# One-core attention block: where the rows of the stacked bf16 q and k are copied from, and where they lie

## The reference, cut to what matters

```python
x = L0_attn_x                                  # (4, 512, 256) f32
xn = _layernorm(x, axis=-1)
qkv = xn @ Wqkv.T + bqkv                       # 16 heads of 16
q, k, v = to_heads(...); q = _rope(q); k = _rope(k)
att = softmax(where(causal, q @ k.T / sqrt(16), -inf)) @ v
s = att @ Wo.T + bo
g = _silu(einsum('btd,rde->bte', xn, factors) / sqrt(8) + bias)
return x + s * g
```

## Time and profile before

| | |
|---|---|
| median of 3 runs | 281.85 us (279.93 to 281.97) |
| profiled execution, first to last instruction | 280.9 us |
| DMAs of 64 KB to stacks (L343) | 96, of which GpSimd issues 4 |
| DMAs of 128 KB within stacks (L380) | 48 |
| mean granted TensorE clock | 0.918 |

### The profile page before, as it was taken

One profiled execution on the slowest core, in us unless ns is written; L12 is line 12 of the kernel. 1 busy time (PEld: TensorE's weight loads), 2 busy tenths in 40 slices (PEclk: granted clock), 3 DMA queues, 4 the chain that ended last, 5 costly groups with the idle time before them and its releaser, 6 DMA issues.

```text
span 280.9 us, 4735 instructions
## 1 busy us (share of the span) xinstructions
PE 228.2 (81%) x1672; PEld 142.9 (51%) x1672; DVE 201.8 (72%) x623; ACT 139.3 (50%) x259; POOL 118.6 (42%) x85
## 2 busy tenths in 40 slices
PE   6480446878896999999599599997599989999992
PEld 2350333354463665556475375645467546675662
DVE  2879882988977699899657389899145898861125
ACT  1403240022493566598336345678025849748950
POOL 4065780643744413783070156575070890016000
PEclk9986586989999799999999869999599999999998
DMA  6970885830496780267598300067585000002002
GB/s 199 359 245 19 105 101 74 99 55 2 66 100 81 84 124 5 41 81 92 63 105 128 99 0 2 22 93 103 87 103 128 0 3 2 2 1 79 0 2 75
DMA packets 16407, 21.28 MB, mean 76 GB/s; under 512 B 2240, under 2 KB 14912, under 8 KB 15616
## 3 DMA queue, kind: packets, MB, share of 16 engines
q1 hardware_dynamic: 15936, 20.59, 43.6%
q0 software_dynamic: 192, 0.26, 0.7%
q10 hardware_dynamic: 256, 0.13, 0.3%
HBM read 6.16 MB, written 2.10 MB: 29 GB/s over the span
## 4 chain that ended last, share of the span: by engine, by line
PE 36%; DVE 20%; DMA 20%; SPq 13%; ACT 5%; issue 3%; ACTq 2%; DVEq 0%
DMA stack_k<-parts 9%; PE o_ps L416 8%; DVE ring_ps L687 8%; SPq L343 8%; DMA stack_k<-stack_k 7%; PE ring_ps L494 6%; PE ring_ps L470 5%; PE ring_ps L460 5%; SPq L380 4%; PE ring_ps L453 4%; ACT probs L786 3%; DMA xbuf<-x 2%; PE ring_ps L426 2%; PE ring_ps L504 2%; DVE rotated L667 2%
## 5 line engine op out<-in xcount | busy, mean ns | idle before, releaser
L687 DVE CUSTOM_DVE_ANT_0 ring_ps<-ring_ps,later_k 128x512 f32<-128x512 f32 (+3 forms) x224 | 107.1, 541 | 27.3 <-PE ring_ps L470 26.5
L786 ACT ACTIVATE probs<-ring_ps 128x512 f32<-128x512 f32 x160 | 85.6, 613 | 28.6 <-PE ring_ps L504 26.1
L470 PE MATMUL ring_ps<-stack_k,stack_q 96*128 96x512 bf16 (+3 forms) x256 | 64.3, 313 | 18.7 <-DMA stack_k<-stack_k 15.7
L494 PE MATMUL ring_ps<-stack_q,stack_k 98*128 98x512 bf16 (+3 forms) x256 | 60.7, 306 | 4.5 <-DVE rowmax L687 3.8
L470 PEld LDWEIGHTS ring_ps<-stack_k,stack_q 96*128 96x128 bf16 x256 | 22.9, 101 | 39.4 <-issue 22.9
L460 PE MATMUL ring_ps<-wvg_sb,xnT 128*128 128x512 f32 x96 | 32.4, 487 | 11.9 <-DVE wvg_sb L603 11.9
L504 PE MATMUL ring_ps<-ident_bf,later_k 128*128 128x256 bf16 (+1 forms) x160 | 40.8, 255 | 0.0
L416 PE MATMUL o_ps<-probs,vaug 128*17 128x256 f32 (+3 forms) x496 | 36.1, 430 | 0.5 <-ACT probs L786 0.4
L494 PEld LDWEIGHTS ring_ps<-stack_q,stack_k 98*128 98x128 bf16 x256 | 23.1, 99 | 18.3 <-DVE rowmax L687 8.6
L453 PE MATMUL ring_ps<-xnT,wqk_sb 128*128 128x512 f32 x96 | 27.8, 443 | 4.7 <-DVE xnT L612 4.7
L687 DVE DVE_READ_ACCUMULATOR2_ANT rowmax<- 128x1 f32 x224 | 31.3, 140 | 0.0
(11 more groups left out here) (84 smaller groups left out, 303.6 us busy)
## 6 DMA issues: line engine op xcount, KB each, us to landing
stack_q<-stack_q SPq DMA_DIRECT2D x24, 128.0 KB
stack_k<-stack_k SPq DMA_DIRECT2D x24, 128.0 KB
stack_q<-parts SPq DMA_DIRECT2D x46, 64.0 KB
stack_k<-parts SPq DMA_DIRECT2D x46, 64.0 KB
probs<-factors SPq DMA_DIRECT2D x2, 1024.0 KB, 9.7
out<-result SPq DMA_DIRECT2D x8, 256.0 KB, 3.4
xbuf<-x SPq DMA_DIRECT2D x3, 512.0 KB, 8.3
xbuf<-x SPq DMA_DIRECT2D x2, 256.0 KB, 2.9
```

The source lines that it names most:

```text
L470: mm = pe.matmul(ps[:, s * width:(s + 1) * width], qk[b % 2][0][0:DOT_ROWS, h, tile * P:(tile + 1) * P], qk[b % 2][1][0:DOT_ROWS, h, 0:width],
L494: pe.matmul(ps[:, col:col + T - j * P], qk[b % 2][1][0:ROWS, h, j * P:(j + 1) * P], qk[b % 2][0][0:ROWS, h, j * P:T], start=(n == 0), stop ...
L687: last = dve.tensor_tensor_reduce(scores, scores, later_k[:, T - width:], 1.0, LOWEST, ALU.add, ALU.max, rowmax[:, tile, h:h + 1])
L786: act.activation(probs[:, pair % PROB_SLOTS, i % EXP_CHUNKS, :], ps[:, :], ACT.Exp, scale=float(HD) ** -0.5).then_inc(taken[kind], 1)
```

## The change

All 12 blocks of 8 rows that a stack and unit have ("places", `PLACES = 12`) are copied from `parts`; nothing is copied from stack to stack. Where 8 rows of one place were adjacent, they are now four partitions apart: place 4g + r takes rows 32g + r, 32g + r + 4, ... 32g + r + 28. The order of the rows within the 96 changes alike for q and k, so the dot products are the same sums.

```diff
-STACK_DMAS = 2 * 5
+PLACES = len(Q_PARTS) * 2
+STACK_DMAS = 2 * PLACES
+def stack_rows(place):
+    first = 4 * HALF * (place // 4) + place % 4
+    return slice(first, first + 4 * (HALF - 1) + 1, 4)
...
-            row = STACKED_PARTS[n].index(part) * HD
-            if part < 2:
-                signal_of_place = s_placed[part]
-            else:
-                signal_of_place = s_stack[b % PARITIES][u] if (b, u) != (0, 0) else s_first_low
-            for half in range(2):
-                eng.dma_start(qk[b % PARITIES][n][row + half * HALF:row + (half + 1) * HALF,
-                                                  u * UH:(u + 1) * UH, :],
-                              parts[n * UR:(n + 1) * UR, u, part, half, :]
-                              ).then_inc(signal_of_place, 16)
+            placed = s_first_low if (b, u, part) == (0, 0, 2) else s_stack[b % PARITIES][u]
+            for product, held in enumerate(STACKED_PARTS[n]):
+                if held == part:
+                    for half in range(2):
+                        eng.dma_start(qk[b % PARITIES][n][stack_rows(2 * product + half), u * UH:(u + 1) * UH, :],
+                                      parts[n * UR:(n + 1) * UR, u, part, half, :]
+                                      ).then_inc(placed, 16)
...
-                    def repeat(n, part):
-                        sp.wait_ge(s_placed[part], 4 * 16 * (UNITS * b + i + 1))
-                        stack = qk[b % PARITIES][n][:, i * UH:(i + 1) * UH, :]
-                        first, *others = (g * HD for g, held in enumerate(STACKED_PARTS[n]) if held == part)
-                        for row in others:
-                            sp.dma_start(stack[row:row + HD], stack[first:first + HD]).then_inc(stacked, 16)
...
+                    for part in range(3):
+                        if (b, i, part) != (0, 0, 2):
+                            place(sp, b, i, 0, part)
+                            place(sp, b, i, 1, part)
```

More of the change, by code:

```diff
@@ L296, in block_kernel @@
         s_low = sem("low_ready")
-        s_placed = [sem("high_placed"), sem("middle_placed")]
         s_first_low = sem("first_low_placed")
@@ L371, in _ @@
                         sp.wait_ge(done_pe["scores"], count("scores", b - PARITIES, (i + 1) * UP * EXP_CHUNKS - 1))
-                    stacked = s_stack[b % PARITIES][i]
-                    def repeat(n, part):
-                        sp.wait_ge(s_placed[part], 4 * 16 * (UNITS * b + i + 1))
-                        stack = qk[b % PARITIES][n][:, i * UH:(i + 1) * UH, :]
-                        first, *others = (g * HD for g, held in enumerate(STACKED_PARTS[n]) if held == part)
-                        for row in others:
-                            sp.dma_start(stack[row:row + HD], stack[first:first + HD]).then_inc(stacked, 16)
[L382 to L392, removed]
+                    for part in range(3):
+                        if (b, i, part) != (0, 0, 2):
+                            place(sp, b, i, 0, part)
+                            place(sp, b, i, 1, part)
                 elif kind == "project_o":
```

## The result

The median is 263.84 us (four runs, 262.32 to 266.05), beside 280.89 us for the kernel before in the same session (278.00 to 281.97). The ratio is 0.9418, with a 95% interval of 0.9348 to 0.9488: 17.0 us faster. The forecast was 268.6 us. Ratios leave out a few disturbed executions, so they can differ by some thousandths from the quotient of two medians. The profiled execution has a span of 264.2 us and its own time is 266.05.

What follows compares the result with a forecast made beforehand. The prediction took slow filling of the stacks to bound the kernel, with PE waiting 15.7 us for them. A to E sum to 13.2 us: 280.9 to 267.7, plus 0.9 for the median, 268.6 us; range 262 to 279.

Steps and rivals of the forecast that it cites:

- The new copy: A 64 KB copy onto rows four apart: taken as 0.35 us, below SP's issue of 0.655 us; landing about 2.5 us.
- A: Unit (0, 0): stack complete at 40.3, 4.3 us earlier; worth 4.0 us, ends 2.7 and 4.3.
- B: Unit (1, 0): stack ready at 87.5, PE's whole gap of 2.26 closes; worth 2.2 us, ends 1.0 and 2.26.
- C: Unit (2, 0): PE's 3.20 us gap closes until VectorE is late next; worth 2.0 us, ends 1.2 and 3.2.
- D: Batch 3's x, issued after unit (2, 1)'s stacks, goes out 5.1 us earlier; worth 2.9 us, ends 1.5 and 3.07.
- worth nothing: Second units (u = 1): their stacks are ready earlier too, but no one waits for them; 0 us.
- E: Unit (3, 0): filling takes 17.6 us instead of 19.7; worth 2.1 us, ends 1.2 and 3.93, PE still waiting 1.8.
- The 0.9 us that tied the span to the median: Added to the 267.7 us forecast for the profiled execution to give the forecast median of 268.6 us.
- Rival 1: Every unit's copies stay as slow as a place, 0.9 us each: about 8.3 us slower, 290 us; chance 0.12.
- Rival 2: Gaps for stacks close but VectorE takes over; only A and E remain, 6.1 us: 275.7 us; chance 0.15.
- Rival 3: The change does nothing: a copy takes about 0.75 us or units keep their length; 281 to 282 us; chance 0.05.
- some 5 us: Sign expected in the new profile: batch 3's x goes out this long after unit (2, 1) could have ended.

Runs made afterwards that it cites:

- experiment 1: The changed kernel with each copy's 8 destination rows adjacent again, all copies still straight from `parts`: 300.13 us, ratio 1.0642.
- experiment 2: The kernel before with only the rows spread (a place's four apart, a product's two apart), stack-to-stack copies kept: 261.88 us, ratio 0.932.
- before, again: The kernel before, unchanged, run once more for a second profile: 284.03 us in one execution.
- 4, x early: The kernel before with only batch 3's x issued by GpSimd once the result is there, not by SP behind the stacks: 280.07 us, ratio 0.996.
- 6, second units: The change in the second units (u = 1) alone, first units filled as in the kernel before: 275.55 us, ratio 0.9803.
- 7, x held: The changed kernel with SP made to wait for the scores of unit (1, 1) before issuing batch 3's x: 264.22 us, ratio 0.9416.
- 5, first units: The change in the first units (u = 0) alone, second units filled as in the kernel before: 266.55 us, ratio 0.9496.
- after, again: The changed kernel, unchanged, run once more for a second profile: 265.12 us in one execution.
- experiment 8: The kernel of experiment 2 with VectorE's normalisation of batch 1 moved later, to after about 13 of unit (0, 0)'s 22 maxima: 259.37 us, ratio 0.9266.

## Why the prediction was right, and by how much it was off

**The mechanism held.** The step "what holds the repeats is where the bytes lie, not the number of engines" is what experiments 1 and 2 tell apart: the same DMAs with other destination rows give 300.1 or 263.8 us, and copies of copies with other rows give 280.9 or 261.9. For the repeats by themselves it is the 121 and 201 GB/s under experiment 2, with 16 outer rows in both.

The Trainium skill's SBUF — State Buffer (Door 1: The DMA port swizzle) gave an estimate of 1.2 us for eight adjacent rows and 0.3 for rows four apart; by the same rule rows two apart reach four ports, an estimate of 0.6 us. Measured are 0.83 to 0.98 us with adjacent rows, quicker than the page's estimate, and no more than SP's 0.655 at two and at four apart, where the copy itself is hidden; so the order is the page's, and the time of a spread copy was not measured. By the Trainium skill's DMA: Bandwidth & Descriptors (Why a DMA increments its semaphore by 16) a copy with eight outer rows uses eight engines and one with sixteen uses sixteen. That did not decide: the former now move 99 GB/s at a share of 0.35, the latter moved 121 at 1.11.

**The new copy.** "Any value below 0.655 us gives the same result" held: the issue is the pace. Landing was taken as 2.5 us and measured at 2.2 in steady state, 2.56 at the end of unit (0, 0). Unit (0, 0) was to be complete at 40.3 and is at 40.30; unit (3, 0) was to take 17.6 us and takes 17.8 (164.48 to 182.30).

**A and B.** Forecast 4.0 and 2.2, measured 4.97 and 2.64. The maxima of (0, 0) start 4.34 us earlier, the upper end of A. Another 0.8 us come from there to the first place of (1, 0), 24.37 us against 25.15. That is no more than executions of one kernel differ: the second profiles have 23.68 and 25.70, the longer one at a lower mean clock (0.74 against 0.78). In B the gap of 2.26 closed, and with it goes the stretch at the lower clock behind it, 91 to 95 us: PE's busy time there falls from 38.98 to 37.99 us.

**C and D, where a term was mis-sized:** 4.9 forecast, 7.83 measured. The working took D from PE's gap ("the gap of 3.07 is the limit: 2.9"), shortened C to 2.0 for VectorE's end at 136.36, and left the clock out of the sum. VectorE's statistics of batch 3's x, before and in the changed kernel, cut the stretch from the first place of (2, 0) to that of (3, 0) in two:

```profile
158.17 1.41 DVE L644 BATCH_NORM_STATS2 stats<-xbuf 128x6 f32<-128x256 f32 x4 [4.53 <-DMA xbuf<-x]
```

```profile
143.72 1.40 DVE L630 BATCH_NORM_STATS2 stats<-xbuf 128x6 f32<-128x256 f32 x4
```

"To VectorE" is from the first place of (2, 0) until VectorE is free for these statistics, and "behind" is from their start to the first place of (3, 0). All in us, but for the mean granted clock:

| kernel | PE's wait at (2, 0) | to VectorE | stall for x | behind | clock behind | stretch |
|---|---|---|---|---|---|---|
| before | 3.20 | 41.09 | 4.53 | 21.90 | 0.84 | 67.52 |
| before, again | 3.09 | 40.95 | 4.50 | 22.04 | 0.85 | 67.49 |
| 4, x early | 3.19 | 41.03 | 2.27 | 20.77 | 1.00 | 64.07 |
| 6, second units | 2.65 | 41.87 | 0 | 20.77 | 1.00 | 62.64 |
| 7, x held | 0 | 39.07 | 1.76 | 20.77 | 1.00 | 61.60 |
| 5, first units | 0 | 38.93 | 0 | 20.76 | 1.00 | 59.69 |
| after | 0 | 38.93 | 0 | 20.76 | 1.00 | 59.69 |
| after, again | 0 | 38.94 | 0 | 20.76 | 1.00 | 59.70 |

The stretches behind the statistics, before, in experiment 4 and after:

```profile
158.17:180.07 21.90, 19.21 (x125) 12.33 (x126) 19.22 (x65) 10.99 (x21) 11.87 (x9) 0.84 0.01 2
```

```profile
155.89:176.66 20.77, 18.87 (x136) 11.40 (x135) 18.91 (x65) 13.00 (x25) 11.89 (x9) 1.00 0.06 16
```

```profile
143.72:164.48 20.76, 20.70 (x165) 13.10 (x158) 18.90 (x67) 12.74 (x25) 11.86 (x9) 1.00 0.01 2
```

So C was sized rightly: VectorE comes to its statistics 2.16 us earlier, where 2.0 was forecast, and not the whole 3.20 of PE's gap. D was not. VectorE's stall passes on in full, 4.53 us and not the 3.07 of PE's gap, which had been set as its upper end; experiments 4 and 7 show the same, with nothing but x's moment changed (a stall 2.26 us shorter, and 1.76 of it put back). Behind it come another 1.14 us, in which the same work takes 20.76 us instead of 21.90. It takes longer only where the clock is at the lower level, as it is behind the stall in both profiles of the kernel before, and that is the clock that the prediction did not count. 2.16 + 4.53 + 1.14 = 7.83. What runs on VectorE there is row maxima, and PE's idle time shows only the part of VectorE's lateness that the ring of PSUM banks had not covered; this reason for the difference between 4.53 and 3.07 is argued, not shown. Whether the lower clock comes from the stall is not shown by itself either: it follows stalls of 4.5 us and more (experiment 1, too, with 5.54) and none of 2.27 or less.

The second units were "worth nothing" in the prediction, and given the first units that is so in this stretch: in experiment 5, x leaves 33.52 us after the first place of (2, 0), in the changed kernel 33.51, both right behind the result, and all of C and D is there. Only while the first units are filled the old way does a shorter queue of second units bring x out earlier (experiment 6: 36.46 us after that first place, before 38.90). VectorE comes later there, at 41.87, beside a stretch at the lower clock from 133 to 137 us that neither profile of the kernel before has.

One thing is not settled. Experiment 4 moves the stretch by 3.45 us and the median by 0.8. The stretch repeats within 0.03 us in both kernels that were profiled twice, which speaks for variation elsewhere. Experiment 6's median moves by 4.8 and its stretch by 4.88, but that agreement says little: its profiled execution was the fastest of its four and is 9.7 us shorter than that of before. How much of D an average execution sees is left open.

**E.** 2.1 forecast, 1.84 measured; PE still waits 2.09 us where 1.8 was expected. After it the changed kernel loses 0.7 us to the end.

**The sum.** 13.2 us forecast, 16.7 between the profiles, 17.05 between the medians. The forecast lay 3.9 us short of the gain, most of it in D (5.7 us for 2.9). The distance from 268.6 to 263.84 is 3.5 us from the terms (2.9 of it C and D), 0.96 from the median of before, which was 280.89 instead of 281.85 with more runs, and 0.35 between profiles and medians. The 0.9 us that tied the span to the median was no property of a run: every run that lists both has its span 1.8 us below its time, so the profiled execution of before was a long one, about 282.7.

**The rivals.** Rival 1 is what adjacent rows do (300.1 us, 0.98 us per copy, above its deciding point of 0.75); the change's rows are on the other side of that point. Rival 2 did not decide the change, but its mechanism is real: where the stacks come early enough, in experiment 2, PE waits 4.26 us behind VectorE's normalisation at (0, 0), and experiment 8's median is 2.5 us lower. Rival 3 fell with the ratio. Of what was to be seen in the profile, nearly all was there: waits only at (0, 0) and (3, 0), 5.2 us instead of some 4, and 99 GB/s for about 100. x left at 138.30, right behind the stores; their two issues reached from 136.44 to 138.26, across the end of the result at 137.86, so it was the result that held x and not the queue. That is 1.9 us behind the last issue of unit (2, 1), as the prediction's own working has it (144.0 and 146.3), and not the "some 5 us" of its list.

## What to carry to other kernels

When DMAs within SBUF are slow, compare their GB/s and busy share with those of a load onto all partitions before counting DMAs: full engines at a third of the rate pointed here to rows that lie badly, and moving the rows was the whole gain. Then look at the issuing queue: once copies are quick, each further DMA costs its issue (0.655 us here), and fewer, larger copies may win again. When a stall sits on a busy engine, price its removal by that engine's stall, not by the shorter gap that its neighbour shows, and add what the clock gives back behind it.

## What the runs showed of the hardware

- A 64 KB copy within SBUF onto eight rows took 0.83 to 0.98 us with adjacent rows; with rows two or four apart it kept up with issues 0.655 us apart, at a smaller DMA share (0.35 to 0.36 at 98 GB/s, against 0.52 at 83 GB/s in experiment 1).
- 128 KB copies from 16 rows to 16 rows of a stack moved 121 GB/s at a DMA share of 1.11 with adjacent rows, and 201 GB/s at 0.90 with rows two apart (experiment 2).
- Four normalisations of 128x256 on VectorE took 1.38 us with GpSimd idle, 3.18 us with GpSimd's arithmetic beside part of it, 4.65 beside its memset, and 6.46 us beside the memset and the arithmetic that followed at once (experiment 2). Where an instruction stands relative to another engine's can matter more than the instruction itself.
- The same stretch of work, with VectorE busy for 19 of its us, took 20.75 to 20.77 us at the full granted clock in nine profiles, and 21.90 to 22.04 us at a mean of 0.84 to 0.85 in the other three (the kernel before, twice, and experiment 1).
